# Global attention: two transposes of the unit three back stand behind each score matmul, in place of a row of scores and a row of transposes

## The chip, the cores and the metric

One core of a Trainium2 chip runs the whole program. The metric is device time in microseconds. The engines named here are TensorE (PE; its weight loads are listed apart as PEld), VectorE (DVE), ScalarE (ACT), GpSimd (POOL) and SyncE (SP).

## What is computed

An input x of 2 x 32 x 32 x 64 goes through three layers: neighbourhood attention with an MLP, a global attention, and a scanned stack of routed feed-forward and attention steps. The change touches the second. Its core in the reference:

```python
def _L1_attn_ref(x, Wq, Wk, Wv, Wu, bu):      # x: 2 images, 1024 tokens each, 64 channels
    h = 8; scale = e ** (-0.25)
    q = (x @ Wq).reshape(b, t, h, e) * scale
    k = (x @ Wk).reshape(b, t, h, e) * scale
    v = (x @ Wv).reshape(b, t, h, e)
    dot = jnp.einsum('bqhe,bkhe->bhqk', q, k)
    att = jax.nn.softmax(dot, axis=-1)
    out = jnp.einsum('bhqk,bkhe->bqhe', att, v).reshape(b, t, h * e)
    return out @ Wu + bu
```

It is called as t = t + _L1_attn_ref(_ln_t(t), ...).

## The kernel before

**Units.** The 8 heads are taken in 4 pairs (NPAIR), with 32 units in each (UP): a unit is one tile of 128 queries of one head (lane) of one image against its 1024 keys. Pair 0 and pair 3 are written out, pairs 1 and 2 are a loop on the engines. All engines run a function glob_pair with a step counter i, and each engine does in step i its share of several units, shifted against each other:

- TensorE (lines 781 to 850), in this order: the scores of unit i, 4 matmuls in half precision of 512 columns (two parts of the query's split times two halves of the keys, line 793), into one of two score buffers of two banks; the 8 transposes of unit i - 3 (TURN = 3, line 806), the first four into the bank LO, the others into HI; one key tile of the value product of a group of 8 units (line 820; none in steps 3, 11, 19 and 27, two tiles in steps 2, 10, 18 and 26); in steps 1, 3, 8, 10, 17, 19, 24 and 26 a projected piece of later queries (line 753; pair 0 has 8, 9, 10 and 11 in place of the first four, pair 3 only the first four); in every eighth step the output product (line 846).
- VectorE (lines 1583 to 1630): the negated row maximum of unit i (L1595), the low part of the piece projected in the step before, if there was one (L1563), the copy of HI of unit i - 3 to PT (L1607), and in steps 6, 14, 22 and 30 the scaling and adding of a group's output (L1613 to L1623).
- ScalarE (lines 1150 to 1173): the exponential of unit i (L1155), the high part of a piece (L1129), the copy of LO of unit i - 2 to PT (L1167), which TensorE transposes in step i + 1.

**What waits for what.** Each engine runs its list in order and waits on counters. Scores of unit i wait until the exponential of unit i - 2 has read their buffer (exped). The maximum waits for the last score matmul (scored), the exponential for the maximum (maxed) and for the transposes that still read its prob buffer. The transposes of a unit wait for its exponential, the first into LO for ScalarE's copy of the unit before (lo_drained), the first into HI for VectorE's (hi_drained). A projection waits until the piece before it has left the bank (piece_drained, counted by VectorE's low part).

The stage stands beside the end of the first layer in the first steps of pair 0 (mlp, layer norm, turn_norm), and a second kind of attention later in the program has code of its own (pe_attention) that the change leaves alone.

Of the kernel before, what the change touches and what calls it, by code (L numbers as in the profile page):

```python
# [37 lines left out]
P = 128  # L38
B, HH, WW, C = 2, 32, 32, 64
TOK = HH * WW  # L40
NT = TOK // P
BLK = 512
NB = TOK // BLK
# [61 lines left out]
def build(nc, a, out):  # L105
    ctx = ExitStack()
    with ctx:
        def sb(name, shape, dt=F32):
            return ctx.enter_context(nc.sbuf_tensor(name, shape, dt))
# [6 lines left out]
        LO, HI, OB, YB = PS[:, 4, :], PS[:, 5, :], PS[:, 6, :], PS[:, 7, :]  # L116


        ident = sb("ident", [P, P])
# [47 lines left out]
        aS = sb("aS", [P, B * TOK], F16)  # L167
        aT = sb("aT", [C, B * TOK])
        prob = sb("prob", [P, 4, TOK])
# [10 lines left out]
        qS = sb("qS", [P, 2, 2, B * TOK], F16)  # L180
# [78 lines left out]
        def core(name):  # L259
            return {k: sem(f"{name}_{k}") for k in  # L260
                    ("scored", "biased", "maxed", "exped", "inverted", "scaled", "lo_turned", "hi_turned",
                     "lo_drained", "hi_drained", "out_summed", "out_drained", "y_filled", "y_drained")}
# [11 lines left out]
        c1 = core("glob")  # L274
# [24 lines left out]
        scores2 = [PS[:, 2 * k:2 * k + 2, :].rearrange("p a b -> p (a b)") for k in range(2)]  # L299
# [45 lines left out]
        def side_wait(e, key):  # L345

            n = order[key]
            who = SIDE[n][2]
            e.wait_ge(side_drained[who], sum(w == who for _, _, w in SIDE[:n + 1]))
# [73 lines left out]
        UP, GP = 2 * B * GRP, 2 * B  # L423
# [32 lines left out]
        def pieces_at(i, pair, last):  # L456
            return [m for m, t in enumerate(steps_of(pair, last)) if t == i]

        def pieces_before(i, pair, last):

            return sum(t < i for t in steps_of(pair, last))

        def product(pair, k, e):
            return pair * k if isinstance(pair, int) else e.snap(pair * k)
# [63 lines left out]
        def _(pe):  # L528
# [100 lines left out]
            for j in range(WW):  # L629
                bank, slot = 4 + j // 9, j % 9  # L630
                mm = pe.matmul(PS[0:WW, bank, slot * NH0 * REL:(slot + 1) * NH0 * REL],
                               shift[:, :, :].rearrange("c a m -> c (a m)")[:, WW - 1 - j:2 * WW - 1 - j],
                               rpbT[:, :], start=True, stop=True)
# [114 lines left out]
            def project(pair, n, bank):  # L748

                _, lane, blk = PIECES[n]  # L750
                for part in range(2):
                    w = wqk[:, part, bass.ds(pair * 2 + lane, 1), :, :]
                    m = pe.matmul(bank, w.rearrange("p h a c -> p (h a c)"), aS[:, blk * BLK:(blk + 1) * BLK],  # L753
                                  start=(part == 0), stop=(part == 1))
                m.then_inc(piece_filled, 1)
# [18 lines left out]
            def glob_pair(pair, steps=range(UP), cur=True, prev=True, last=False, beside=None):  # L774

                bu, bg, bp = (product(pair, k, pe) for k in (UP, GP, NPC))
                nxt = pair + 1 if isinstance(pair, int) else pe.snap(pair + 1)
                before = pair - 1 if isinstance(pair, int) else pe.snap(pair - 1)

                def live(index):  # L780
                    return cur if index >= 0 else prev

                for i in steps:
                    if cur:
                        if i in (0, UP // B):
                            pe.wait_ge(piece_drained, bp + (HALF if i == 0 else NPC))
                            pe.sem_inc(gate, 1)
                        if i >= 2 or prev:
                            pe.wait_ge(c1["exped"], bu + (i - 1))
                        lane, q0, k0 = i % 2, i // 2 * P, i // (UP // B) * TOK  # L790
                        for part in range(2):
                            for j in range(NB):
                                mm = pe.matmul(scores2[i % 2][:, j * BLK:(j + 1) * BLK], qS[:, part, lane, q0:q0 + P],  # L793
                                               aS[:, k0 + j * BLK:k0 + (j + 1) * BLK],
                                               start=(part == 0), stop=(part == 1))
                        mm.then_inc(c1["scored"], 1)
                    u = i - TURN
                    if live(u):
                        pe.wait_ge(c1["exped"], bu + (u + 1))
                        for half, bank, turned, drained in ((0, LO, "lo_turned", "lo_drained"),  # L800
                                                            (1, HI, "hi_turned", "hi_drained")):
                            if u >= 1 or prev:
                                pe.wait_ge(c1[drained], bu + u)
                            for k in range(4):
                                kt = 4 * half + k
                                tr = pe.transpose(bank[:, k * P:(k + 1) * P],  # L806
                                                  prob[:, u % 4, kt * P:(kt + 1) * P], ident[:, :])
                            tr.then_inc(c1[turned], 1)
                    g = (i - SUM) // GRP
                    k = i - SUM - GRP * g  # L810
                    if live(g) and k < NT - 1:
                        if k == 0:
                            pe.wait_ge(c1["lo_drained"], bu + GRP * (g + 1))
                            pe.wait_ge(c1["hi_drained"], bu + GRP * (g + 1))
                            if g >= 1 or prev:
                                pe.wait_ge(c1["out_drained"], bg + g)
                        for kt in (k, k + 1)[:2 if k == NT - 2 else 1]:
                            for lane in range(2):
                                cols = slice(64 * lane, 64 * lane + 64)
                                mm = pe.matmul(OB[cols, :], V[:, g % GP // 2 * NT + kt, cols],  # L820
                                               PT[:, g % 2, lane, kt, :], start=(kt == 0), stop=(kt == NT - 1))
                        if kt == NT - 1:
                            mm.then_inc(c1["out_summed"], 1)
                    for m in pieces_at(i, pair, last) if cur else ():
                        if isinstance(pair, int) and pair == 0 and m == 0:
                            side_wait(pe, ("a", 1, 0))
                            side_wait(pe, ("a", 1, 1))

                        pe.wait_ge(piece_drained, bp + (HALF + m))
                        g = (i - PROJ - 1) // GRP  # L830
                        if not pieces_at(i - 1, pair, last) and live(g):
                            pe.wait_ge(c1["y_drained"], bg + (g + 1))
                        pe.sem_inc(gate, 1)
                        project(pair if m < HALF else nxt, (HALF + m) % NPC, YB)
                    g = (i - PROJ) // GRP
                    if (i - PROJ) % GRP == 0 and live(g):
                        pe.wait_ge(c1["out_drained"], bg + (g + 1))
                        if cur:
                            pe.wait_ge(piece_drained, bp + (HALF + pieces_before(i, pair, last)))
                        pe.sem_inc(gate, 1)  # L840
                        if g >= 1 or prev:
                            pe.wait_ge(c1["y_drained"], bg + g)
                            pe.sem_inc(gate, 1)
                        p = pair if g >= 0 else before
                        for j in range(QT):
                            mm = pe.matmul(YB[:, j * P:(j + 1) * P], OT[:, g % 2, j * P:(j + 1) * P],  # L846
                                           wu1[:, bass.ds(p, 1), :, :].rearrange("p n l c -> p (n l c)"),
                                           start=True, stop=True)
                        mm.then_inc(c1["y_filled"], 1)
                    if beside:  # L850
                        beside(i)

            glob_pair(0, prev=False, beside=rest_of_stage1)
            with pe.Fori(1, NPAIR - 1) as pair:
                glob_pair(pair)
            glob_pair(NPAIR - 1, last=True)

            def turn_state(blk):
# [108 lines left out]
            for blk in range(B * NB):  # L967
                which, bank = (("lo", LO), ("hi", HI))[blk % 2]
# [878 lines left out]
```

## Time and profile before

| | us |
|---|---|
| three runs | 735.18, 743.02, 764.6 |
| median | 743.02 |
| the profiled execution | 735.33 |
| its span on the core | 733.5 |
| TensorE busy in it | 636.1 (87%) |
| VectorE busy | 465.0 (63%) |
| ScalarE busy | 386.3 (53%) |
| global attention, first to last start of a score matmul | 171.6 to 561.1 |

The profile's groups of instructions are named by source line, output and inputs. A matmul's duration reaches to the end of its drain, so matmuls overlap, and the time from one start to the next is what one costs the stream. "Idle before" is the time that the engine stood still just before an instruction, with what released it.

### The profile page before, as it was taken

The page shows a single profiled execution, that of the slowest core. Times are in us where ns is not written, and L with a number is a line of the kernel's source. Part 1 is how long each engine was busy: PE and PEld are TensorE (multiplying, and loading weights), DVE is VectorE, ACT ScalarE, POOL GpSimd, SP SyncE. Part 2 cuts the span into 40 slices and gives each one's busy share as a digit, 9 for nine tenths or more (in the row PEclk, how much of TensorE's full clock was granted, in tenths as well). Part 3 has the DMA queues.
Part 4 walks back from the last instruction along what each step waited for, and adds up shares of the span by engine and source line. Part 5 has one row for each costly group of instructions (what it writes and reads, how often), then busy time and mean ns, then how long its engine had stood idle before and what let it go on. Part 6 is the DMA issues. An engine that isn't in the chain of part 4 may idle for free.

```text
span 733.5 us, 10440 instructions
## 1 busy us (share of the span) xinstructions
PE 636.1 (87%) x3631; PEld 337.6 (46%) x3632; DVE 465.0 (63%) x799; ACT 386.3 (53%) x683; POOL 49.8 (7%) x100
## 2 busy tenths in 40 slices
PE   7999989969689999999999999999998735478862
PEld 5445644635445555555555555555554311144311
DVE  5754473553966676667676766776768445699343
ACT  3553567235666566656666666666655022466130
POOL 5111331130000000000000000000000000000000
PEclk9995898556999999999999999999999867699976
DMA  4000000000000000000000000000000000000001
GB/s 95 1 1 1 1 1 1 1 0 1 1 0 1 1 1 1 1 1 1 0 0 0 0 0 0 1 1 1 0 1 1 1 9 1 12 1 1 1 0 29
DMA packets 9506, 3.19 MB, mean 4 GB/s; under 512 B 8820, under 2 KB 9079, under 8 KB 9463
## 3 DMA queue, kind: packets, MB, share of 16 engines
q1 hardware_dynamic: 8182, 2.61, 1.5%
q8 instruction: 27, 0.44, 0.2%
q10 hardware_dynamic: 1281, 0.01, 0.1%
q14 instruction: 16, 0.13, 0.1%
HBM read 2.09 MB, written 0.52 MB: 4 GB/s over the span
## 4 chain that ended last, share of the span: by engine, by line
PE 73%; DVE 12%; issue 9%; ACT 3%; POOL 2%; DMA 1%; SPq 0%; DVEq 0%; POOLq 0%; ACTq 0%
PE PS L820 15%; PE PS L793 15%; PE PS L806 13%; PE PS L674 4%; PE PS L662 3%; PE PS L846 2%; PE PS L481 2%; PE PS L753 2%; PE PS L688 2%; PE PS L493 2%; PE PS L505 2%; PE PS L946 2%; DVE negm L1595 2%; PE PS L554 1%; PE PS L580 1%
## 5 line engine op out<-in xcount | busy, mean ns | idle before, releaser
L1595 DVE TENSOR_REDUCE negm<-PS 128x1 f32<-128x1024 f32 x128 | 156.5, 1222 | 120.1 <-PE PS L793 120.0
L1155 ACT ACTIVATE prob<-PS,negm 128x1024 f32<-128x1024 f32 x128 | 142.8, 1116 | 43.6 <-DVE negm L1595 43.6
L806 PE MATMUL PS<-ident,prob 128*128 128x128 f32 x1024 | 135.8, 274 | 10.5 <-DVE PT L1607 10.3
L806 PEld LDWEIGHTS PS<-ident,prob 128*128 128x128 f32 x1024 | 119.8, 141 | 39.0 <-DVE PT L1607 13.2
L820 PE MATMUL PS<-PT,V 128*64 128x512 f32 x512 | 134.3, 617 | 0.0
L793 PE MATMUL PS<-aS,qS 128*128 128x512 f16 x512 | 133.9, 384 | 0.0
L1167 ACT ACTIVATE PT<-PS 128x512 f32<-128x512 f32 x128 | 76.6, 598 | 106.9 <-PE PS L806 106.3
L1607 DVE COPY PT<-PS 128x512 f32<-128x512 f32 x128 | 87.0, 680 | 5.1 <-PE PS L806 5.1
L793 PEld LDWEIGHTS PS<-aS,qS 128*128 128x128 f16 x512 | 44.7, 99 | 95.7 <-issue 52.1
L1084 ACT ACTIVATE prob<-sbias,negm 128x320 f32<-128x320 f32 (+1 forms) x64 | 34.2, 537 | 38.8 <-DVE negm L1507 38.2
L1274 POOL TENSOR_TENSOR rstd<-var,minus_half 128x8 f32<-128x8 f32 x8 | 13.2, 1644 | 464.2 <-DVE var L1378 464.2
L674 PE MATMUL PS<-ident,prob 128*128 128x128 f32 x176 | 41.5, 353 | 0.4 <-ACT prob L1084 0.4
L820 PEld LDWEIGHTS PS<-PT,V 128*64 128x64 f32 x512 | 27.3, 135 | 30.0 <-issue 29.8
L662 PE MATMUL PS<-k0S,q0S 32*128 32x320 f16 (+1 forms) x128 | 32.5, 348 | 6.9 <-DVE negm L1507 6.3
L312 DVE COPY PT<-PS 128x384 f32<-128x384 f32 (+1 forms) x32 | 16.7, 522 | 30.8 <-PE PS L674 30.7
L1507 DVE CUSTOM_DVE_ANT_0 sbias<-PS,PT 128x320 f32<-128x320 f32 (+1 forms) x64 | 28.6, 457 | 8.6 <-PE PS L662 8.4
L674 PEld LDWEIGHTS PS<-ident,prob 128*128 128x128 f32 x176 | 22.7, 170 | 21.4 <-issue 15.9
L987 ACT ACTIVATE prob<-PS,negm 128x1024 f32<-128x1024 f32 x16 | 17.8, 1114 | 16.7 <-DVE negm L1332 16.7
L1129 ACT ACTIVATE qS<-PS 128x512 f16<-128x512 f32 x36 | 21.2, 598 | 8.1 <-PE PS L753 7.6
L1155 ACT ACTIVATION_READ_ACCUMULATOR prob<-PS,negm 128x1 f32 x128 | 25.3, 198 | 0.0
L753 PE MATMUL PS<-aS,wqk 128*128 128x512 f16 x64 | 20.3, 411 | 5.0 <-DVE qS L1563 3.6
L481 PE MATMUL PS<-kS,qS 128*128 128x512 f16 x64 | 16.4, 381 | 9.0 <-ACT prob L987 7.7
(173 smaller groups left out, 655.0 us busy)
## 6 DMA issues: line engine op xcount, KB each, us to landing
xall<-in_x_dram SPq DMA_DIRECT2D x2, 256.0 KB, 4.4
out_dram<-x SPq DMA_DIRECT2D x4, 128.0 KB, 2.1
w<-in_L_attn_Wq_dram SPq DMA_DIRECT2D x2, 128.0 KB, 2.5
w<-in_L_attn_Wk_dram SPq DMA_DIRECT2D x2, 128.0 KB, 2.7
w<-in_L_attn_Wv_dram SPq DMA_DIRECT2D x2, 128.0 KB, 2.7
fc<-in_L_conv_fc_w_dram SPq DMA_DIRECT2D x2, 64.0 KB, 2.5
wu<-in_L_attn_Wu_dram SPq DMA_DIRECT2D x2, 64.0 KB, 2.3
w1s<-in_L_ffn_ffn_w_dram SPq DMA_DIRECT2D x2, 64.0 KB, 2.1
```

The costliest lines, as they stand in the source:

```text
L481: mm = pe.matmul(scores2[u % 2][:, j * BLK:(j + 1) * BLK], qS[:, part, lane, q0:q0 + P], kS[:, lane, j * BLK:(j + 1) * BLK], start=(part = ...
L662: mm = pe.matmul(PS[:, u % 2, 0:rows * WW], q0S[hr, img, part, t * P:(t + 1) * P], k0S[hr, img, first * WW:(first + rows) * WW], start=(pa ...
L674: tr = pe.transpose(bank[:, n * P:(n + 1) * P], prob[:, u % 3, n * P:(n + 1) * P], ident[:, :])
L753: m = pe.matmul(bank, w.rearrange("p h a c -> p (h a c)"), aS[:, blk * BLK:(blk + 1) * BLK], start=(part == 0), stop=(part == 1))
L793: mm = pe.matmul(scores2[i % 2][:, j * BLK:(j + 1) * BLK], qS[:, part, lane, q0:q0 + P], aS[:, k0 + j * BLK:k0 + (j + 1) * BLK], start=(pa ...
L806: tr = pe.transpose(bank[:, k * P:(k + 1) * P], prob[:, u % 4, kt * P:(kt + 1) * P], ident[:, :])
L820: mm = pe.matmul(OB[cols, :], V[:, g % GP // 2 * NT + kt, cols], PT[:, g % 2, lane, kt, :], start=(kt == 0), stop=(kt == NT - 1))
L1084: act.activation(prob[:, i % 3, 0:w], sbias[:, i % 3, 0:w], ACT.Exp, bias=negm[:, i % 4:i % 4 + 1], scale=-1.0).then_inc(c0["exped"], 1)
L1155: act.activation(prob[:, i % 4, :], scores2[i % 2], ACT.Exp, bias=negm[:, i % 4:i % 4 + 1], scale=1.0, accum_out=sums[:, i // GRP, (i % GR ...
L1167: act.activation(PT[:, g % 2, lane, 0:4, qt * P:(qt + 1) * P], LO.rearrange("p (k q) -> p k q", k=4), ACT.Copy).then_inc(c1["lo_drained"], 1)
L1595: dve.tensor_reduce(negm[:, i % 4:i % 4 + 1], scores2[i % 2], AX.X, ALU.max, negate=True)\
L1607: dve.tensor_copy(PT[:, g % 2, lane, 4:8, qt * P:(qt + 1) * P], HI.rearrange("p (k q) -> p k q", k=4)).then_inc(c1["hi_drained"], 1)
```

## The change

The four score matmuls of unit i and the eight transposes of unit i - 3 are issued by two small functions, score(n) and turn(kt), and a loop over n = 0 to 3 issues score(n), turn(2n), turn(2n + 1). The counters are raised by the same instructions as before: scored by the fourth score matmul, LO's and HI's by the fourth and the eighth transpose. The wait for LO's copy stands ahead of turn(0), thus behind score(0), and the wait for HI's copy ahead of turn(4), behind score(2). The wait for the exponential of unit i - 3 is ahead of score(0). Where a step has only one of the two kinds (the first three steps and those behind the last unit), its order is as before.

```diff
--- before.py
+++ after.py
@@ -787,25 +787,37 @@
                             pe.sem_inc(gate, 1)
                         if i >= 2 or prev:
                             pe.wait_ge(c1["exped"], bu + (i - 1))
-                        lane, q0, k0 = i % 2, i // 2 * P, i // (UP // B) * TOK
-                        for part in range(2):
-                            for j in range(NB):
-                                mm = pe.matmul(scores2[i % 2][:, j * BLK:(j + 1) * BLK], qS[:, part, lane, q0:q0 + P],
-                                               aS[:, k0 + j * BLK:k0 + (j + 1) * BLK],
-                                               start=(part == 0), stop=(part == 1))
-                        mm.then_inc(c1["scored"], 1)
                     u = i - TURN
                     if live(u):
                         pe.wait_ge(c1["exped"], bu + (u + 1))
-                        for half, bank, turned, drained in ((0, LO, "lo_turned", "lo_drained"),
-                                                            (1, HI, "hi_turned", "hi_drained")):
-                            if u >= 1 or prev:
-                                pe.wait_ge(c1[drained], bu + u)
-                            for k in range(4):
-                                kt = 4 * half + k
-                                tr = pe.transpose(bank[:, k * P:(k + 1) * P],
-                                                  prob[:, u % 4, kt * P:(kt + 1) * P], ident[:, :])
+
+                    def score(n):
+
+                        lane, q0, k0 = i % 2, i // 2 * P, i // (UP // B) * TOK
+                        part, j = n // NB, n % NB
+                        mm = pe.matmul(scores2[i % 2][:, j * BLK:(j + 1) * BLK], qS[:, part, lane, q0:q0 + P],
+                                       aS[:, k0 + j * BLK:k0 + (j + 1) * BLK],
+                                       start=(part == 0), stop=(part == 1))
+                        if n == 2 * NB - 1:
+                            mm.then_inc(c1["scored"], 1)
+
+                    def turn(kt):
+
+                        bank, turned, drained = ((LO, "lo_turned", "lo_drained"),
+                                                 (HI, "hi_turned", "hi_drained"))[kt // 4]
+                        if kt % 4 == 0 and (u >= 1 or prev):
+                            pe.wait_ge(c1[drained], bu + u)
+                        tr = pe.transpose(bank[:, kt % 4 * P:(kt % 4 + 1) * P],
+                                          prob[:, u % 4, kt * P:(kt + 1) * P], ident[:, :])
+                        if kt % 4 == 3:
                             tr.then_inc(c1[turned], 1)
+
+                    for n in range(2 * NB):
+                        if cur:
+                            score(n)
+                        if live(u):
+                            turn(2 * n)
+                            turn(2 * n + 1)
                     g = (i - SUM) // GRP
                     k = i - SUM - GRP * g
                     if live(g) and k < NT - 1:
```

On TensorE, in pair 0, the projection of step 26 and then all of step 27 (before; L753 is the projection, L793 a score matmul, L806 a transpose of prob; xN at a row's end says how many in a row):

```order
L753 MATMUL PS<-aS,wqk 128x512 [waits glob_piece_drained,glob_y_drained]
L753 MATMUL PS<-aS,wqk 128x512
L793 MATMUL PS<-aS,qS 128x512 [waits glob_exped]
L793 MATMUL PS<-aS,qS 128x512 x3
L806 MATMUL PS<-ident,prob 128x128 [waits glob_lo_drained,glob_exped]
L806 MATMUL PS<-ident,prob 128x128 x3
L806 MATMUL PS<-ident,prob 128x128 [waits glob_hi_drained]
L806 MATMUL PS<-ident,prob 128x128 x3
```

The same place with the change, where L798 is the score matmul and L810 the transpose:

```order
L753 MATMUL PS<-aS,wqk 128x512 [waits glob_piece_drained,glob_y_drained]
L753 MATMUL PS<-aS,wqk 128x512
L798 MATMUL PS<-aS,qS 128x512 [waits glob_exped]
L810 MATMUL PS<-ident,prob 128x128 [waits glob_lo_drained]
L810 MATMUL PS<-ident,prob 128x128
L798 MATMUL PS<-aS,qS 128x512
L810 MATMUL PS<-ident,prob 128x128 x2
L798 MATMUL PS<-aS,qS 128x512
L810 MATMUL PS<-ident,prob 128x128 [waits glob_hi_drained]
L810 MATMUL PS<-ident,prob 128x128
L798 MATMUL PS<-aS,qS 128x512
L810 MATMUL PS<-ident,prob 128x128 x2
```

The fourth score matmul, which raises scored, stood at the fourth place of the step and stands now at the tenth; the fifth transpose, which waits for glob_hi_drained, stood at the ninth and stands at the eighth, ahead of that score matmul.

On VectorE nothing moves. Its list at that place, in both kernels (with the line numbers of before), is the maximum of step 26, the copy of HI of step 26, the maximum of step 27, the low part of the piece of step 26, and the copy of HI of step 27:

```order
L1595 TENSOR_REDUCE negm<-PS 128x1 [waits glob_scored]
L1607 COPY PT<-PS 128x4x128 [waits glob_hi_turned]
L1595 TENSOR_REDUCE negm<-PS 128x1 [waits glob_scored]
L1563 SCALAR_TENSOR_TENSOR qS<-PS,qS 128x512 [waits glob_piece_high_made]
L1607 COPY PT<-PS 128x4x128 [waits glob_hi_turned]
```

The low part stands between the maximum and the copy that the fifth transpose of step 28 waits for.

## Rows read from the trace of the kernel before

**Rows 1.** windows: busy us of PE, PEld, DVE, ACT, POOL, clock, DMA

```profile
382.00:479.00 97.00, 96.32 (x550) 50.98 (x550) 67.72 (x88) 61.16 (x106) 0.00 (x0) 1.00 0.00 0
```

**Rows 2.** waits, 284 to 479 us: sum, times, longest

```profile
DVE negm L1595 <- PE PS L793: 58.1, 51, 2.3
ACT PT L1167 <- PE PS L806: 50.5, 56, 1.8
...
PE PS L806 <- DVE PT L1607: 1.4, 4, 0.3
```

**Rows 3.** timeline, TensorE: start, us, what, xcount [idle before]

```profile
452.17 1.03 PE L793 MATMUL PS<-aS,qS 128*128 128x512 f16 x4
453.04 1.04 PE L806 MATMUL PS<-ident,prob 128*128 128x128 f32 x8
453.91 1.03 PE L793 MATMUL PS<-aS,qS 128*128 128x512 f16 x4
454.77 0.60 PE L806 MATMUL PS<-ident,prob 128*128 128x128 f32 x4
455.71 0.65 PE L806 MATMUL PS<-ident,prob 128*128 128x128 f32 x4 [0.34 <-DVE PT L1607]
456.30 1.08 PE L820 MATMUL PS<-PT,V 128*64 128x512 f32 x4
```

**Rows 4.** timeline, TensorE's weight loads around 453.8 us

```profile
453.80 0.21 PEld L793 LDWEIGHTS PS<-aS,qS 128*128 128x128 f16 x2
```

**Rows 5.** timeline, TensorE, a plain step and the next start

```profile
457.31 1.04 PE L793 MATMUL PS<-aS,qS 128*128 128x512 f16 x4
458.18 1.04 PE L806 MATMUL PS<-ident,prob 128*128 128x128 f32 x8
459.15 1.08 PE L820 MATMUL PS<-PT,V 128*64 128x512 f32 x4
460.16 0.38 PE L846 MATMUL PS<-wu,OT 128*128 x1
```

**Rows 6.** timeline, TensorE, a step with projection, without value product

```profile
427.33 1.04 PE L793 MATMUL PS<-aS,qS 128*128 128x512 f16 x4
...
429.07 0.59 PE L753 MATMUL PS<-aS,wqk 128*128 128x512 f16 x2
429.50 1.03 PE L793 MATMUL PS<-aS,qS 128*128 128x512 f16 x4
```

**Rows 7.** timeline, VectorE in the plain step

```profile
458.38 1.22 DVE L1595 TENSOR_REDUCE negm<-PS 128x1 f32<-128x1024 f32 x1 [1.00 <-PE PS L793]
459.52 0.68 DVE L1607 COPY PT<-PS 128x512 f32<-128x512 f32 x1
```

**Rows 8.** timeline, ScalarE in the plain step

```profile
458.82 0.60 ACT L1167 ACTIVATE PT<-PS 128x512 f32<-128x512 f32 x1 [0.79 <-PE PS L806]
```

**Rows 9.** timeline, VectorE beside rows 3

```profile
454.38 0.68 DVE L1563 SCALAR_TENSOR_TENSOR qS<-PS,qS 128x512 f16<-128x512 f32 x1
454.98 0.68 DVE L1607 COPY PT<-PS 128x512 f32<-128x512 f32 x1
```

**Rows 10.** timeline, VectorE, the output's scaling and the next maximum

```profile
463.95 0.19 DVE L1613 RECIPROCAL weight<-sums 128x8 f32<-128x8 f32 x1
...
465.71 1.22 DVE L1595 TENSOR_REDUCE negm<-PS 128x1 f32<-128x1024 f32 x1
```

**Rows 11.** timeline, pair 0, projections in a row

```profile
203.89 0.68 DVE L1563 SCALAR_TENSOR_TENSOR qS<-PS,qS 128x512 f16<-128x512 f32 x1
...
204.71 0.59 PE L753 MATMUL PS<-aS,wqk 128*128 128x512 f16 x2 [1.13 <-DVE qS L1563]
```

**Rows 12.** timeline, pair 0 beside the layer norm

```profile
186.37 0.66 PE L806 MATMUL PS<-ident,prob 128*128 128x128 f32 x4 [1.01 <-DVE PT L1607]
...
187.55 1.22 DVE L1595 TENSOR_REDUCE negm<-PS 128x1 f32<-128x1024 f32 x1
```

**Rows 13.** timeline, TensorE, rows 3 one pair earlier

```profile
356.97 0.66 PE L806 MATMUL PS<-ident,prob 128*128 128x128 f32 x4 [0.34 <-DVE PT L1607]
```

## The prediction

> **What bounds the kernel now.** I read the stretches first, then the waits, then single units of the order. A unit below is one 128-query tile of one head: 32 in a head pair, 128 in all. In the steady part of the global attention TensorE is busy 96.32 of 97 us at a granted clock of 1.00 [rows 1]. There VectorE waits 58.1 us for score matmuls and ScalarE 50.5 us for transposes, while TensorE waits 1.4 us in sum for VectorE's copy of a transposed half [rows 2]. So TensorE's own stream sets the end, and the question is whether the new order shortens it, or makes it wait.
>
> *Prices in the stream.* Four score matmuls take from 453.91 to 454.77, so **s** = 0.216 us from one start to the next; eight transposes followed by scores take 453.04 to 453.91, so **d** = 0.109 us each [rows 3]. The weight load of a score matmul starts at 453.80, with the last transpose, and its matmul follows 0.11 us later [rows 4]: a transpose takes d whether a transpose or a score matmul stands behind it. A score matmul takes s whether a score matmul or a transpose stands behind it: 457.31 to 458.18 is 4s [rows 5].
>
> *Step lengths L*, from a unit's first score matmul to what follows the step: 2.85 us for a plain step (scores, transposes, one key tile of the value product), the usual case (457.31 to 460.16, where an output product happens to follow) [rows 5]; 2.17 for a step without value product but with a projection [rows 6]; 1.74 with neither [rows 3].
>
> **The change, part by part.** It adds and removes no instruction: 4 score matmuls and 8 transposes a unit, 4s + 8d = 1.74 us before and after. TensorE's stream alone is worth 0. What moves is when it signals and when it needs something.
>
> 1. *The row maximum starts later.* Before, the fourth score matmul starts at 3s; now six transposes stand ahead of it, 3s + 6d. VectorE's maximum starts 1.07 us after the step's start in a plain step (457.31, 458.38) [rows 5, 7], so 1.07 + 6d = **1.72** after.
> 2. *The fifth transpose comes earlier.* It writes HI and waits until VectorE has copied out the unit before. It stood at 4s + 4d = 1.30; now at 3s + 4d = **1.08**.
> 3. *LO is finished earlier* (2s + 4d = 0.87 against 1.30). ScalarE, which copies LO, already waits for transposes [rows 2] and its copy isn't what anybody waits for: worth 0. The transpose at the front waits for LO's copy of the step before; that copy starts at 458.82 and is done by 459.42, 0.7 us ahead of the next step at 460.16 [rows 5, 8], with or without the change: 0 too, but a score matmul's length (0.65) less cover than before.
>
> Points 1 and 2 together take 0.65 + 0.22 = **0.87 us of slack** from VectorE's chain: maximum, (on some steps) the low part of a projected piece, then the copy of HI. Its prices: 1.14 us from the maximum's start to what follows (458.38 to 459.52) and 0.68 for the copy [rows 7]; 0.60 for the low part (454.38 to 454.98) [rows 9]; 0.05 from the copy's end (454.98 + 0.68) to the transpose (455.71) [rows 3, 9]; 0.06 for a weight load that is no longer hidden (four transposes ahead of a value product took 0.59 from 455.71, and 0.97 - 4d = 0.53 in the plain step) [rows 3, 5]. So after the change the fifth transpose is late by
>
> 1.72 + 1.14 + 0.68 + 0.11 - (L + 1.08) = 2.57 - L, plus 0.60 where a low part stands between; before it was 1.70 - L (plus 0.60).
>
> The formula for the old order gives 1.70 + 0.60 - 1.74 = 0.56 for the short step with a low part. The trace has it: 454.77 to 456.30 is 1.53 where the plain step has 0.97 [rows 3, 5]. Now by kind of step (numbers are i in a pair's 32 steps):
>
> - plain step, nothing between: 2.57 - 2.85, 0.28 us in hand, no wait.
> - plain step with low part (4, 9, 20, 25): late **0.32**, before -0.55.
> - no value product, projection (3, 19): late **0.40**.
> - no value product, no projection, low part (11, 27): 1.43 against 0.56, **+0.87**.
> - after the output's scaling on VectorE (6, 14, 22, 30), which takes 1.76 (463.95 to 465.71) [rows 10] and pushes the next maximum: 1.72 + 1.14 + 0.60 + 1.76 + 1.14 + 0.68 + 0.11 - (2 x 2.85 + 1.08) = **0.37**, before -0.50. (Work that is followed by other work on VectorE costs 0.60 a copy, by [rows 9].)
>
> Behind a late transpose stands the fourth score matmul, so this unit's maximum is late as well. That is why the waits add up and aren't caught up: nothing on TensorE is idle otherwise. That matmuls do not overtake a waiting one shows at 455.71, behind which the value product starts only at 456.30 [rows 3]. The Trainium skill ("TensorE: Matmul & The Clock Gate", Part 2) says it too: only weight loads are pulled ahead, "The MATMULs themselves stay in program order".
>
> Sum. Pairs 1 and 2: 4 x 0.32 + 2 x 0.40 + 2 x 0.87 + 4 x 0.37 = 5.30 each. Pair 3 projects only in its first half: 2 x 0.32 + 0.40 + 0.87 + 2 x (2.57 - 1.74 = 0.83) + 4 x 0.37 = 5.05. Pair 0, late part: 0.40 + 3 x 0.32 + 0.87 + 0.37 = 2.60. Pair 0 projects in steps 8 to 11 in a row, and each projection waits for the low part of the one before, which stands behind the maximum (203.89, 204.71) [rows 11]: a maximum 0.65 later makes three steps longer by 0.65, 1.95. Its steps 4 to 7 carry a layer norm and are VectorE's: a transpose let go at 186.37 gives scores by 186.37 + 0.06 + 2d + 0.42 = 187.07, and VectorE is free only at 187.55 [rows 12]: 0. One transpose behind the last scores: before late 0.36, after 1.01, 0.65. Total 10.60 + 5.05 + 2.60 + 1.95 + 0.65 = **20.9 us**.
>
> The profiled execution took 735.33 us, its span 733.5. 735.3 + 20.9 = **756 us**. The median of the three runs shown, 743.02, stands 1% above the profiled one, and the highest at 764.6: the changed kernel may scatter upward likewise. Small errors matter little: about 45 late places, 0.05 us of error in each is 2.3 us. An own range is 751 to 763.
>
> **A rule that speaks against this.** The trace shows d both ahead of a transpose and ahead of a score matmul [rows 3, 4]. The Trainium skill (same page, "LDWEIGHTS (loading the stationary operand)") gives a load as columns / 1.2, 107 ns for 128, and in "Back-to-back issue gap" 56 ns for a matmul of 128 columns; by these, back-to-back transposes would be held by their loads, and the interleaving would hide three loads a unit. By that rule the sum would have some 20 us less in TensorE's stream. The row on the load at 453.80 doesn't bear it out, since the half-precision load behind it should have let the score matmul start sooner.
>
> **The rivals.**
>
> - *Loads get hidden* (the rule above). As a mechanism of this kernel: a transpose ahead of a score matmul costs s / 4 = 0.054 (128 columns at the speed of 512) instead of d. Three a unit, 125 units: -20.6. But VectorE's dates then come earlier as well: at each of the 45 late places the steps ahead are 0.11 to 0.28 shorter, about +7. 735.3 + 20.9 - 20.6 + 7 = **743**, no difference. Against: [rows 4]. 0.05. Only with the waits gone too would it be 735.3 - 20.6 = **715**, faster; it decides if less than 6 us of the waits come. 0.03.
> - *The small waits are absorbed*: my chain is 0.4 us too long, so that only the short steps wait. 6 places x 0.87 + 2 x 0.43 + 1.95 + 0.65 = 8.7, **744**, not slower by what can be told. For it: each small term is a difference of sums near 3.6 us. Against: the same sums hit the 0.56 of the old order to 0.01. 0.09.
> - *Each switch costs*: the trace has a transpose that takes 0.20 instead of 0.109, ahead of a value product (0.97 - 7d) [rows 5]. If each of three more returns to a score matmul a unit cost that 0.093, 35 us, of which the longer steps give back the small waits: 735.3 + 35 + 9 = **779**. Against: one such return costs 0 [rows 4]. 0.05.
> - *The forecast*, 756: 0.78.
>
> **How the numbers follow.** About 2%, some 15 us, is what a measurement of this kernel can tell from no change. Slower: the forecast and the costly switch, 0.83 less a little for the forecast's lower edge, 0.82. Same: 743 and 744, and that edge, 0.15. Faster: 0.03. The range 742 to 776 takes in the load rival and the absorbed waits below, and upward most of the way to 779 and the scatter.
>
> **What would show it.** In the changed trace: TensorE's spacing of 4s + 8d unchanged without waits; a pair's period, now 98.74 us (356.97 to 455.71) [rows 3, 13], becomes 104.0; the maximum starts 1.7 us after the step's first score matmul; transposes waiting for VectorE's HI copy in 12 places a pair, the two after the short steps the longest, at 1.4 us. Wrong it is if score matmuls follow a transpose in under 0.1 us, or if the waits stay at two a pair.

## The result

The changed kernel takes 764.96 us (median of 5 runs, 756.04 to 778.55) against 743.02 (median of 5, 735.18 to 764.6): 1.0295 times the time before, 95% interval 1.0216 to 1.0374, slower. The fastest runs differ by 756.04 - 735.18 = 20.9 us. Some executions of a kernel run as a whole at a lower granted clock and take longer; a ratio with an interval leaves them out, so that it can differ from the quotient of two medians, which are over all runs.

The profiled execution of the changed kernel took 778.55 us; its first layer, whose code the change doesn't touch, ran at a lower granted clock and took longer. So the two traces are compared by stages. Busy time of PE, PEld, DVE, ACT and POOL, the granted clock and DMA in three stretches of the trace before (up to the first score matmul of the global attention, the global attention, the rest):

```profile
0.00:171.00 171.00, 150.82 (x948) 85.55 (x949) 91.36 (x267) 82.36 (x161) 44.92 (x97) 0.81 0.05 11
171.00:562.00 391.00, 380.99 (x2180) 206.80 (x2180) 273.46 (x347) 247.33 (x425) 1.64 (x1) 0.99 0.00 1
562.00:733.50 171.50, 104.24 (x507) 45.23 (x505) 100.22 (x186) 56.63 (x98) 3.27 (x2) 0.82 0.03 6
```

and of the changed one:

```profile
0.00:190.00 190.00, 173.51 (x943) 94.74 (x945) 92.19 (x267) 81.19 (x159) 45.04 (x97) 0.67 0.05 10
190.00:606.00 416.00, 392.75 (x2188) 216.14 (x2188) 274.28 (x346) 243.59 (x428) 1.64 (x1) 0.99 0.00 1
606.00:776.70 170.70, 102.28 (x503) 45.67 (x501) 100.48 (x187) 56.18 (x97) 3.27 (x2) 0.83 0.03 6
```

From the first to the last start of a score matmul of the global attention, the trace before has 171.6 to 561.1, 389.5 us, the changed one 194.7 to 605.3, 410.6: **21.1 us more**, at a clock of 0.99 in both. What comes behind it is as long as it was (171.5 and 170.7). The first score matmul stands at 194.7 instead of 171.6: the other 23 us are the first layer's, at 0.67 instead of 0.81, and 1 us is given back behind the stage (the spans differ by 43.2).

Who waits for whom in the changed kernel, from 307 to 515 us, two whole head pairs (sum, times, longest); it answers to [rows 2]:

```profile
ACT prob L1167 <- DVE negm L1607: 76.8, 65, 1.8
DVE negm L1607 <- PE PS L798: 68.4, 56, 2.3
...
PEld PS L810 <- DVE PT L1619: 16.6, 24, 1.6
...
ACT PT L1179 <- PE PS L810: 9.2, 16, 0.7
...
PE PS L810 <- DVE PT L1619: 5.6, 8, 1.2
```

Two more lines of the same view of the kernel before, from 284 to 479 us:

```profile
ACT prob L1155 <- DVE negm L1595: 18.0, 52, 0.9
...
PEld PS L806 <- DVE PT L1607: 2.3, 4, 0.6
```

TensorE and its weight loads waited for VectorE's copy of HI 4 times in two pairs, and now wait 24 times, 12 a pair. ScalarE's exponential waits 76.8 us for the maximum instead of 18.0, and its LO copy waits 9.2 us for transposes instead of 50.5. What TensorE did in the short step without value product (27) and the one behind it (28) in pair 2, answering to [rows 3]:

```profile
489.66 0.38 PE L798 MATMUL PS<-aS,qS 128*128 128x512 f16 x1
489.88 0.38 PE L810 MATMUL PS<-ident,prob 128*128 128x128 f32 x2
490.10 0.38 PE L798 MATMUL PS<-aS,qS 128*128 128x512 f16 x1
...
490.97 0.38 PE L798 MATMUL PS<-aS,qS 128*128 128x512 f16 x1
...
491.40 0.38 PE L798 MATMUL PS<-aS,qS 128*128 128x512 f16 x1
...
492.27 0.38 PE L798 MATMUL PS<-aS,qS 128*128 128x512 f16 x1
493.86 0.44 PE L810 MATMUL PS<-ident,prob 128*128 128x128 f32 x2 [1.21 <-DVE PT L1619]
494.13 0.38 PE L798 MATMUL PS<-aS,qS 128*128 128x512 f16 x1
...
495.67 0.39 PE L798 MATMUL PS<-aS,qS 128*128 128x512 f16 x1
```

The spacing is the old one: 489.66 to 491.40 is 1.74 us for four score matmuls and eight transposes, and a score matmul starts 0.22 ahead of its two transposes and the next one 0.22 behind their start. In step 28 the third score matmul starts at 492.27, so the fifth transpose could go at 492.49; it starts at 493.86, with the fourth score matmul (494.13) behind it. VectorE beside it, answering to [rows 7, 9]:

```profile
491.38 1.23 DVE L1607 TENSOR_REDUCE negm<-PS 128x1 f32<-128x1024 f32 x1 [2.32 <-PE PS L798]
492.52 0.68 DVE L1575 SCALAR_TENSOR_TENSOR qS<-PS,qS 128x512 f16<-128x512 f32 x1
493.12 0.68 DVE L1619 COPY PT<-PS 128x512 f32<-128x512 f32 x1
...
497.40 1.23 DVE L1607 TENSOR_REDUCE negm<-PS 128x1 f32<-128x1024 f32 x1 [1.03 <-PE PS L798]
```

The maximum starts at 491.38, 1.72 us after the step's first score matmul at 489.66 (in the plain step behind, 495.67 and 497.40, 1.73); low part and copy follow as before, and the copy ends at 493.80, 0.06 ahead of the transpose.

### The profile page after: what moved, and what is told of

It is laid out like the page before. It is cut to its first block, busy times and chain, and to the rows that moved or that the text cites. A ratio compares the mean times of both kernels' runs of the same rounds, so it can differ in the third digit from the quotient of the medians.

```text
span 776.7 us, 10441 instructions
## 1 busy us (share of the span) xinstructions
PE 668.5 (86%) x3631; PEld 356.6 (46%) x3632; DVE 467.0 (60%) x799; ACT 381.0 (49%) x683; POOL 50.0 (6%) x100
## 4 chain that ended last, share of the span: by engine, by line
PE 62%; DVE 22%; issue 11%; ACT 1%; POOL 1%; DMA 1%; DVEq 0%; SPq 0%; POOLq 0%; ACTq 0%
PE PS L810 10%; PE PS L832 9%; PE PS L798 9%; DVE negm L1607 6%; PE PS L674 5%; DVE PT L1619 5%; PE PS L662 4%; PE PS L688 2%; DVE qS L1575 2%; PE PS L858 2%; PE PS L571 2%; PE PS L481 2%; PE PS L493 2%; PE PS L505 2%; PE PS L554 2%
## 5 line engine op out<-in xcount | busy, mean ns | idle before, releaser
L810 PE MATMUL PS<-ident,prob 128*128 128x128 f32 x1024 | 198.1, 277 | 22.7 <-DVE PT L1619 20.2
L798 PE MATMUL PS<-aS,qS 128*128 128x512 f16 x512 | 194.6, 383 | 0.0
L810 PEld LDWEIGHTS PS<-ident,prob 128*128 128x128 f32 x1024 | 140.4, 142 | 84.3 <-DVE PT L1619 40.2
L798 PEld LDWEIGHTS PS<-aS,qS 128*128 128x128 f16 x512 | 50.3, 99 | 62.3 <-issue 58.6
L674 PE MATMUL PS<-ident,prob 128*128 128x128 f32 x176 | 49.5, 408 | 0.1
L662 PE MATMUL PS<-k0S,q0S 32*128 32x320 f16 (+1 forms) x128 | 39.2, 409 | 3.6 <-DVE negm L1519 3.1
L674 PEld LDWEIGHTS PS<-ident,prob 128*128 128x128 f32 x176 | 26.5, 195 | 27.3 <-issue 19.9
L753 PE MATMUL PS<-aS,wqk 128*128 128x512 f16 x64 | 20.5, 414 | 6.9 <-DVE qS L1575 5.5
L1575 DVE SCALAR_TENSOR_TENSOR qS<-PS,qS 128x512 f16<-128x512 f32 x36 | 24.2, 682 | 0.4 <-ACT qS L1141 0.3
```

What stands on the lines that cost most here:

```text
L662: mm = pe.matmul(PS[:, u % 2, 0:rows * WW], q0S[hr, img, part, t * P:(t + 1) * P], k0S[hr, img, first * WW:(first + rows) * WW], start=(pa ...
L674: tr = pe.transpose(bank[:, n * P:(n + 1) * P], prob[:, u % 3, n * P:(n + 1) * P], ident[:, :])
L810: tr = pe.transpose(bank[:, kt % 4 * P:(kt % 4 + 1) * P], prob[:, u % 4, kt * P:(kt + 1) * P], ident[:, :])
L1575: ins = dve.scalar_tensor_tensor(qS[:, 1, lane, toks], bank, scales[1], qS[:, 0, lane, toks], ALU.mult, ALU.subtract)
```

## Experiments

A pair's period is the time from the first maximum of pair 1 to the first of pair 2, 98.74 us in the kernel before. It's the same in pairs 1 and 2 of each kernel to 0.1 us, and doesn't see the first layer. The changed kernel:

```profile
299.42 1.23 DVE L1607 TENSOR_REDUCE negm<-PS 128x1 f32<-128x1024 f32 x1 [0.75 <-PE PS L798]
...
403.36 1.23 DVE L1607 TENSOR_REDUCE negm<-PS 128x1 f32<-128x1024 f32 x1 [0.75 <-PE PS L798]
```

103.94 us. The single runs of the orders and of VectorE's variants, 736.76 to 787.68 us in the whole, can't be compared among each other, since the first layer alone differs by up to 30 us (last section); the period can. The two rivals that I tested against "lost slack" are "each switch between score matmul and transpose costs" (loads or switches that the alternation makes dearer), and hidden loads, which would make it shorter.

**The order on TensorE, in doses.** Four orders of the same twelve instructions, which lose different amounts of slack. In place of the change's loop:

```diff
-                    for n in range(2 * NB):
-                        if cur:
-                            score(n)
-                        if live(u):
-                            turn(2 * n)
-                            turn(2 * n + 1)
+                    ns, nt = 0, 0
+                    for what in "ssttttsstttt":
+                        if what == "s" and cur:
+                            score(ns)
+                        if what == "t" and live(u):
+                            turn(nt)
+                        ns, nt = ns + (what == "s"), nt + (what == "t")
```

with "ststststtttt" for the second and "sttsttststtt" for the third. Two rows of each:

> Order of a step: two score matmuls, four transposes, two score matmuls, four transposes. Theory (lost slack): the last score matmul starts 4d = 0.44 us later than before the change, and the fifth transpose stands where it stood, at 4s + 4d; so 0.44 us of slack is lost, not 0.87. Only the two short steps of a pair are late by more: a pair's period 98.74 + 2 x 0.44 = 99.6 us, with 2 waits a pair of about 1.0 us, and the global attention 3 to 5 us longer than before. Rival (each switch between a score matmul and a transpose costs, and the 5.2 us a pair of the change come from its six additional switches a unit): two additional switches, 98.74 + 5.2 / 3 = 100.5 us. Rival (loads get hidden): not above 98.7.

```profile
292.42 1.22 DVE L1608 TENSOR_REDUCE negm<-PS 128x1 f32<-128x1024 f32 x1 [0.33 <-PE PS L798]
...
392.04 1.23 DVE L1608 TENSOR_REDUCE negm<-PS 128x1 f32<-128x1024 f32 x1 [0.40 <-PE PS L798]
```

99.62 us, as the slack rule gives, and not 100.5. The global attention was 5.0 us longer between its first and last maximum (393.7 against 388.7), where I had expected 3 to 5. One transpose between:

> Order of a step: score, one transpose, three times, then score and the other five transposes. Same number of switches as the change. Theory (lost slack): the last score matmul is 3d = 0.33 us later, the fifth transpose still behind all scores, at 4s + 4d; 0.33 us of slack lost: period 98.74 + 2 x 0.33 = 99.4 us. Rival (each switch costs): the same as the change, 103.9 us.

```profile
272.27 1.23 DVE L1608 TENSOR_REDUCE negm<-PS 128x1 f32<-128x1024 f32 x1 [0.33 <-PE PS L798]
...
371.66 1.22 DVE L1608 TENSOR_REDUCE negm<-PS 128x1 f32<-128x1024 f32 x1 [0.39 <-PE PS L798]
```

99.39 us. This order alternates as often as the change does, and costs 0.65 us a pair where the change costs 5.20. The one with the last score matmul one transpose earlier:

> Order of a step: the change's, but the last score matmul stands one transpose earlier (score, 2, score, 2, score, 1, score, 3), still behind the fifth transpose, which waits for HI. Theory (lost slack): 5d + s = 0.76 us lost: 4 x (0.76 - 0.55) + 2 x (0.76 - 0.47) + 2 x 0.76 + 4 x (0.76 - 0.50) = 3.98 us a pair, period 102.7 us, the waits at the same 12 places but each 0.11 shorter. Rival (each switch costs): 103.9 us.

```profile
305.34 1.23 DVE L1608 TENSOR_REDUCE negm<-PS 128x1 f32<-128x1024 f32 x1 [0.64 <-PE PS L798]
...
407.96 1.23 DVE L1608 TENSOR_REDUCE negm<-PS 128x1 f32<-128x1024 f32 x1 [0.64 <-PE PS L798]
```

102.62 us against the 102.7 expected. Four points of slack lost, 0.33, 0.44, 0.76 and 0.87 us, cost 0.65, 0.88, 3.88 and 5.20 us a pair: over 0.5 us the other ten places join the two short ones. A cost for each switch can't give 0.65 and 5.20 for the same number of switches.

**The same order only where there is slack.**

```diff
...
+                    apart = not (i in (0, 1, 2, 5, 8, 10, 13, 16, 17, 18, 21, 24, 26, 29)
+                                 and not (isinstance(pair, int) and pair == 0 and i < 13))
...
+                    for what in "sssstttttttt" if apart else "sttsttsttstt":
```

> The change's order only in steps 0, 1, 2, 5, 8, 10, 13, 16, 17, 18, 21, 24, 26 and 29 of a pair (in pair 0 only from 13 on), the old order in the others: the 14 steps behind which the old order has over 0.65 us of slack to the next fifth transpose, and 0.22 for its own. Theory (lost slack): the same 14 of 32 interleaved units cost nothing: a pair's period stays at 98.74 us, with only the two waits of 0.56 of the old order. Rival (each switch costs): 14 of 32 parts of 5.2 us, 101.0 us. Rival (the alternation slows the chip's clock or the engine): above 98.74 in some measure.

```profile
273.15 1.23 DVE L1610 TENSOR_REDUCE negm<-PS 128x1 f32<-128x1024 f32 x1 [0.98 <-PE PS L798]
...
371.89 1.23 DVE L1610 TENSOR_REDUCE negm<-PS 128x1 f32<-128x1024 f32 x1 [1.05 <-PE PS L798]
```

98.74 us, to the hundredth what it was before: 14 of 32 units interleaved cost nothing, and gain nothing. With the unchanged spacing in the trace of the change, that settles both rivals: a switch costs nothing here, and no hidden load shortens the stream.

**VectorE's part of the chain.** The low part behind the copy of HI, with the change's order on TensorE:

```diff
+                    def low():
                         for m in pieces_at(i - 1, pair, last) if cur else ():
                             ...
+                    early = isinstance(pair, int) and pair == 0 and i <= 12
+                    if early:
+                        low()
                     u = i - DRAIN - 1
                     if live(u):
                         ...
+                    if not early:
+                        low()
```

> The change's order on TensorE; on VectorE the low part of a projected piece stands behind the copy of HI instead of ahead of it (from step 13 of pair 0 on). Theory (VectorE's chain to the HI copy is what is late): the four waits behind a low part in a plain step (0.32 each) go, the two at the short steps fall from 1.43 to about 0.83; others stay: the period falls from 103.94 to about 101.5 us. Rival (each switch costs, or the interleaved scores are what takes longer): stays at 103.9.

```profile
289.23 1.23 DVE L1607 TENSOR_REDUCE negm<-PS 128x1 f32<-128x1024 f32 x1 [0.74 <-PE PS L798]
...
390.72 1.22 DVE L1607 TENSOR_REDUCE negm<-PS 128x1 f32<-128x1024 f32 x1 [0.75 <-PE PS L798]
```

101.49 us. The order on TensorE is the change's, and 2.45 us of the 5.20 are gone by moving one instruction of VectorE. Its waits in two pairs:

```profile
PEld PS L810 <- DVE PT L1623: 10.4, 16, 1.0
...
PE PS L810 <- DVE PT L1623: 3.2, 8, 0.6
```

16 in place of 24, the longest 1.0 us. The same edit on the kernel before:

> The kernel before, on VectorE the low part behind the copy of HI (from step 13 of pair 0 on). Theory (the only waits of the old order are the two of 0.56 us a pair behind a low part in a short step): they go (1.70 - 1.74 is under zero), a period of 98.74 - 1.12 = 97.6 us, some 3 us less in the whole, 0.5%: too little to be told from no change by the times alone. Rival (those waits have another cause): 98.7.

```profile
278.21 1.23 DVE L1595 TENSOR_REDUCE negm<-PS 128x1 f32<-128x1024 f32 x1 [0.33 <-PE PS L793]
...
375.84 1.22 DVE L1595 TENSOR_REDUCE negm<-PS 128x1 f32<-128x1024 f32 x1 [0.40 <-PE PS L793]
```

97.63 us: the two waits that the old order had are gone. In the whole 733.02 to 748.02 us in four runs against 743.26 to 764.12 in seven of before, too near for a verdict on times.

**The copy ahead of the maximum**, with the change's order on TensorE (the lines of the HI copy moved up ahead of tensor_reduce):

> The change's order on TensorE; on VectorE the copy of HI stands ahead of the row maximum of the step instead of behind it. HI of unit i - 3 is complete 1.94 us after the step's start, so the copy is done at 2.7 and the fifth transpose of the next step (L + 1.08) never waits for it. Theory (the waits of the change sit in VectorE's chain to that copy, which ran through the late maximum): the 12 waits a pair for the HI copy go. The maximum itself is then 0.8 us later (2.54 instead of 1.72), the exponential ends at about 4.95 and ScalarE's LO copy at 5.65, so that copy becomes late in front of the first transpose two steps on, where two steps are shorter than that (5.0 and 4.6 us around the steps without value product): the period falls from 103.94 to about 102, with waits for ScalarE in place of waits for VectorE. Rival (each switch costs): 103.9.

```profile
313.25 1.21 DVE L1613 TENSOR_REDUCE negm<-PS 128x1 f32<-128x1024 f32 x1
...
414.85 1.21 DVE L1613 TENSOR_REDUCE negm<-PS 128x1 f32<-128x1024 f32 x1
```

```profile
PEld PS L798 <- ACT prob L1167: 18.4, 20, 1.3
...
PEld PS L810 <- ACT PT L1179: 7.9, 20, 0.9
...
PE PS L810 <- ACT PT L1179: 2.3, 4, 0.6
```

101.60 us. Not one wait for VectorE's copy is left in pairs 1 and 2, which is what the chain as the cause asks for; but others came in their place, so this run alone doesn't show that the period goes back to 98.74 without them. The runs above carry that. I had the waits' new kind half right: the LO copy is late at 20 places in the two pairs, but the larger part, 18.4 us, are score matmuls that wait for the exponential of two units back. In pair 0 this order is worse than the change (109.9 us to the first maximum of pair 1 against 102.8), which I had not worked out. Its trace puts that into the three steps between the maxima of steps 9 and 12, 6.74, 6.61 and 6.59 us long against 4.24, 4.12 and 4.12 with the change: each projection waits for the low part, which now stands behind the copy and the maximum,

```profile
233.53 0.99 PE L753 MATMUL PS<-aS,wqk 128*128 128x512 f16 x2 [2.73 <-DVE qS L1575]
```

and in each of the three steps the granted clock fell to its lower level, 1.2 GHz, for 3.4 us behind such a wait of 2.6 to 2.7 us. With the change these waits were 1.8 to 1.9 us, and the clock stayed at 2.4.

**A version that beats both.** [rows 5] have 0.20 us for the last transpose ahead of a value product instead of 0.109, and a visit with one tile takes 1.01 us of value product, where the second tile of a visit adds 0.86. Fewer visits should thus be worth more than any order of scores and transposes. On the kernel before, with the low part last (shown is the version with three visits):

```diff
-                    if live(g) and k < NT - 1:
+                    tiles = {0: (0, 1), 3: (2, 3, 4), 6: (5, 6, 7)}.get(k, ())
+                    if live(g) and tiles:
...
-                        for kt in (k, k + 1)[:2 if k == NT - 2 else 1]:
+                        for kt in tiles:
```

First with four visits of two tiles, in steps 0, 2, 4 and 6 of a group:

> The kernel before with the low part last, and the value product's eight key tiles of a group taken two at a time in four steps, in place of one at a time in six and two in one. In the trace of before a visit of one tile costs 0.09 (the transpose ahead of it takes 0.20 instead of 0.109) + 0.48 + 0.53, and a second tile 0.86 more, so each visit saved is worth 0.24 us. Theory (TensorE's stream sets the end as long as the slack holds): three visits less a group, 4 groups a pair: 98.74 - 1.12 - 4 x 0.72 = 94.7 us a pair, some 14 us less in the whole, about 720; if the longer and shorter steps bring waits back, 95 to 97. Rival (a mean over steps doesn't count, the short steps wait): no less than 97.6.

```profile
281.22 1.22 DVE L1596 TENSOR_REDUCE negm<-PS 128x1 f32<-128x1024 f32 x1
...
375.40 1.22 DVE L1596 TENSOR_REDUCE negm<-PS 128x1 f32<-128x1024 f32 x1
```

94.18 us, and in the whole 731.0 us against 749.13, 0.9758 (0.9659 to 0.9856): faster, though the interval leaves open whether by 2%. With three visits:

> As the one before, with two, three and three tiles in three steps of a group: one visit less a group again: 98.74 - 1.12 - 4 x 0.96 = 93.8 us a pair by the stream alone, some 18 us less in the whole; its short steps follow each other in twos, so by the slack rule (1.70 + work between - L) some waits for the exponential or the LO copy may come, up to 1 us a pair. Rival (short steps wait): 97 or more.

> The kernel with two, three and three tiles a visit again: period 93.15 us, 19 us less than before in the global attention, 0.975 of before in the whole.

```profile
275.64 1.23 DVE L1596 TENSOR_REDUCE negm<-PS 128x1 f32<-128x1024 f32 x1 [0.93 <-PE PS L793]
...
368.80 1.23 DVE L1596 TENSOR_REDUCE negm<-PS 128x1 f32<-128x1024 f32 x1 [1.00 <-PE PS L793]
```

93.16 us in the second series and as much in the first. In the whole 724.99 us in the second (721.01 to 744.94) against 764.04 (743.0 to 764.67), 0.9738 (0.9555 to 0.9921), where 2% is open likewise; in the first 739.94 against 749.13, without an interval. From first to last maximum the global attention takes 369.4 us, against 388.7 before and 409.8 with the change.

**The change once more.**

> The changed kernel once more, for a profile in which the first layer isn't disturbed, on the chip of this series: period 103.94 us again, 21 us more than before between the first and the last maximum of the global attention, and about 3% in the whole.

The period was 103.92 and the global attention 21.7 us longer than before between its first and last maximum. The whole was 781.0 us (775.7 to 786.11) against 764.04 (743.0 to 764.67), 1.052 (1.034 to 1.070), more than the 1.0295 of the first series. In this profile too the first layer is what adds: the first maximum comes at 194.8 us, where the trace before has 173.6. The 21.7 against the 21.1 of the first series are told apart by the first three maxima of pair 0, which follow each other in 3.31 and 2.08 us before, in 3.31 and 2.10 here, and in 2.88 and 1.70 in the first trace of the change: there the granted clock rose to its upper level 2.3 us behind the first maximum, and not 3.9 and 4.0 us as in the two others. So 21.7 is the change alone, and 21.1 holds 0.6 that the clock gave back.

## Why the prediction was right

- *TensorE's stream is worth nothing.* Right: s and d measure 0.216 and 0.109 in the changed trace, on both sides of a switch, and 14 interleaved units a pair cost 0.00.
- *The maximum 0.65 later, the fifth transpose 0.22 earlier.* Right: 1.72 and 1.73 us for the maximum, and in step 28 the fifth transpose could go 492.49 - 491.40 = 1.09 us after the first score matmul (1.08). Point 3 calls the 0.65 us that LO's cover loses a score matmul's length; it is that of three, and nothing waited for LO's copy in pairs 1 and 2 all the same.
- *Which places are late, and by how much.* Right for all four kinds in pairs 1 and 2: 12 places a pair. Against before, maxima behind a low part come 0.32 later (forecast 0.32), behind a step with a projection and no value product 0.40 (0.40), behind the output's scaling 0.35 (0.37); the short step's transpose waits 493.86 - 492.49 = 1.37 plus 0.05 of a load, 1.42 (1.43). The period rose by 5.20 (5.30).
- *Pair 3.* From its first to its last maximum it took 4.8 us more (94.3 to 99.1); 5.05 less the 0.37 that stands in front of the first maximum is 4.7.
- *Pair 0 was mis-sized*: from its fourth maximum to the first of pair 1 it took 5.9 us more (89.8 to 95.7) where I had 4.55, or 4.92 with the wait at the start of pair 1. The step that failed is the one that said 0 for steps 4 to 7 and counted only three steps behind them. The maximum of step 8 is set by VectorE in both kernels and doesn't move, but that of step 9 does: the fifth transpose of step 9 waits for the copy of step 8, and its fourth score matmul behind it:

```profile
221.69 0.68 DVE L1619 COPY PT<-PS 128x512 f32<-128x512 f32 x1
...
222.42 0.44 PE L810 MATMUL PS<-ident,prob 128*128 128x128 f32 x2
...
225.20 0.59 PE L753 MATMUL PS<-aS,wqk 128*128 128x512 f16 x2 [1.91 <-DVE qS L1575]
```

In the kernel before, the maximum of step 9 started 1.24 us after its first score matmul:

```profile
197.93 1.02 PE L793 MATMUL PS<-aS,qS 128*128 128x512 f16 x4
...
199.17 1.21 DVE L1595 TENSOR_REDUCE negm<-PS 128x1 f32<-128x1024 f32 x1
```

In the changed one it is 2.07 (221.04 to 223.11), 1.72 and 0.35 of the wait. That makes 0.83 us (2.57 against 1.74 between the maxima of steps 8 and 9). The row at 225.20 shows the first of the projections that wait for the low part, 1.95 forecast for three steps and 0.67, 0.66 and 0.66 measured.
- *The sum*, 20.9 us: 21.1 between the first and last score matmul, 21.7 in the second trace of the change, whose first steps had the clock of before, and 20.9 between the fastest runs. That the last agrees to 0.1 is luck: the runs of one kernel differ by more than 20 us. Against the 21.7 the sum is 0.8 short, about the 0.83 that is missing in pair 0.
- *The absolute number.* 756 was made against a profiled execution of 735.33; the median came at 764.96. The 9 us are not the change's chain, since the stage has its 21 us: the median of before stood 7.7 us above its profiled execution too, and from median to median it is 21.9. They are in the scatter that the runs of both kernels have upward, and the traces put that into the first layer. The range was meant to hold it and did.
- *The load rule of the Trainium skill* ("TensorE: Matmul & The Clock Gate", "LDWEIGHTS (loading the stationary operand)"), by which, as an estimate, the alternation should have saved some 20 us: no run bears that out. The stretch of 1.74 us for twelve instructions is the same in both orders.

## What to carry to other kernels

Interleaving two streams of one engine moves no work, but it moves every signal and every need: write down for each signal by how much it comes later, for each wait by how much it comes earlier, and hold the sum against the slack of the chain between them, place by place, not on average. Here 0.87 us were taken from ten places that had about 0.5 and two that had none, and those 12 of 32 steps paid. The places that pay are those where the producer's step is short or the consumer does something extra, and the engine between them can be reordered too: moving one instruction of it gave back 2.45 of the 5.20 us here.

## What I had not expected of the hardware

The first layer, whose instructions are the same in all kernels here, reaches the first maximum of the global attention at 173.6 us in the trace before and at 196.6 in the changed one. Over the eleven further traces it came between 173.6 and 203.4. That is as much as the change itself is worth, in runs of one or the other, and it follows TensorE's granted clock: the later the first maximum, the less time up to it is on record at the upper level (2.4 GHz), 64.9 us for 173.6 (before and one between), 61.4 for 175.9, 54.6 for 181.5, 51.2 for 182.3, 44.4 for 187.5 (twice), 34.1 for 193.5 (twice) and 194.8, 23.9 for 196.6 (the change), and 17.1 and 13.7 for 203.4. The time on record at the lower level (1.2 GHz), 67.7 us before and 130.8 with the change, doesn't sort the traces so, because it is incomplete: in four of them, the two at 203.4 and the two at 193.5, the first clock on record is that at 87 us, and not at 41 to 43. Yet the matmuls ran slower there. The same four before and in the run with two rows of each:

```profile
45.48 1.88 PE L554 MATMUL PS<-PT,wqk 65*128 65x512 f32 x4
...
48.98 3.62 PE L554 MATMUL PS<-PT,wqk 65*128 65x512 f32 x4
```

The kernel with three visits, traced twice, had its first maximum at 193.5 and at 181.5, so the clock differs from run to run of one code. Whether a kernel's later code has any part in it was not tested and stays open; so does whether the 1.052 of the second series holds any more of the change than the 21.7 us that its trace shows.

A visit of the value product costs 0.24 us over its tiles: eight records of two tiles stand for 1.87 us where four of one tile stand for 1.01, and the transpose ahead takes 0.20. Fewer visits gave back 3.4 and 4.5 us a pair, where 2.9 and 3.8 had been expected, and were the larger lever by far. Some 0.4 of what came in addition is the output product, four times a pair: it takes 0.99 us to the next score matmul behind a value product (460.16 to 461.15 before), and 0.89 behind transposes (297.36 to 298.25 with two tiles a visit).
